# Attention inside a three-layer kernel: four early blocks for the maxima, two of them behind the shifts' transposes, and the values' copy on ACT

## What is computed

```python
q = (x @ Wq + bq).reshape(b, s, HQ, DH).transpose(0, 2, 1, 3)   # HQ = 16 heads, DH = 32
k = x @ Wk + bk                                                # one head of keys for all 16
v = x @ Wv + bv
scores = jnp.einsum('bhsd,btd->bhst', q, k) / scale
attn = jax.nn.softmax(scores, axis=-1)
out = jnp.einsum('bhst,btd->bhsd', attn, v)
out = out.transpose(0, 2, 1, 3).reshape(b, s, HQ * DH)
return out @ Wo + bo
```

## Time and profile before

| | |
|---|---|
| median of 3 runs | 3292.02 us (3288.11 to 3294.11) |
| the profiled execution's own time | 3288.66 us |
| its span, first to last instruction | 3286.9 us |
| attention's groups | from 833 to about 2590 us of the span |
| busy share of the span | PE 86%, DVE 62%, ACT 45%, POOL 67% |
| mean granted clock of TensorE | 0.926 of full speed |

### The profile page before, as it was taken

How to read it: one execution, slowest core, us unless ns; L and a number is a source line. 1 busy time by engine, 2 the same in 40 slices (tenths; PEclk the granted TensorE clock), 3 DMA queues, 4 the chain that set the end, 5 groups by cost and what they waited for, 6 DMA issues and landing times. The chain is left out here.

```text
span 3286.9 us, 50812 instructions
## 1 busy us (share of the span) xinstructions
PE 2812.6 (86%) x15136; PEld 1579.5 (48%) x15136; DVE 2045.0 (62%) x3940; ACT 1481.8 (45%) x2815; POOL 2210.8 (67%) x1392
## 2 busy tenths in 40 slices
PE   7967778398899999999999999999999798777760
PEld 4644444176555454555554544455554355444430
DVE  7943222267788787788787877777875397222222
ACT  3422222153666565566565655665656243222210
POOL 2148888462688787788887877877878222788870
PEclk9989887699999999999999999999999898879885
DMA  6479999894577676676776766757766243999998
GB/s 215 167 210 249 235 243 232 191 278 158 113 161 142 136 159 140 142 153 131 166 142 135 159 138 139 156 116 155 144 124 142 89 166 116 245 235 245 235 197 315
DMA packets 217011, 576.36 MB, mean 175 GB/s; under 512 B 33948, under 2 KB 34972, under 8 KB 192792
## 3 DMA queue, kind: packets, MB, share of 16 engines
q0 software_dynamic: 87296, 343.98, 52.0%
q1 hardware_dynamic: 125208, 220.55, 20.5%
q10 hardware_dynamic: 4224, 8.39, 0.7%
HBM read 230.94 MB, written 155.24 MB: 117 GB/s over the span
## 5 line engine op out<-in xcount | busy, mean ns | idle before, releaser
L1716 DVE TENSOR_REDUCE attention_mx<-attention_pM 128x1 f32<-128x512 f32 x1984 | 1210.8, 680 | 208.7 <-PE attention_pM L1575 192.6
L1520 ACT ACTIVATE attention_prob<-attention_pS 128x512 f32<-128x512 f32 x2048 | 1035.0, 631 | 565.9 <-PE attention_pS L1562 471.3
L1461 POOL TENSOR_TENSOR attention_pair<-attention_prob 128x1024 f32<-128x1024 f32 x380 | 949.5, 2507 | 195.6 <-ACT attention_prob L1520 184.0
L1562 PE MATMUL attention_pS<-attention_qT,prep_kT 128*128 128x512 f32 x2048 | 842.0, 417 | 25.3 <-issue 16.7
L1575 PE MATMUL attention_pM<-prep_kT,attention_qT 96*128 96x512 f32 x1984 | 808.3, 410 | 0.0
L1562 PEld LDWEIGHTS attention_pS<-attention_qT,prep_kT 128*128 128x128 f32 x2048 | 389.2, 191 | 365.8 <-issue 178.0
L1600 PE MATMUL attention_pO<-attention_prob,attention_v 128*32 128x512 f32 x4096 | 492.5, 598 | 0.0
L629 POOL DMA_INDIRECT sum<-experts_res,c_table x256 | 403.7, 1577 | 106.7 <-issue 76.6
L1575 PEld LDWEIGHTS attention_pM<-prep_kT,attention_qT 96*128 96x128 f32 x1984 | 378.5, 192 | 110.4 <-DVE attention_mx L1716 44.4
L755 DVE TENSOR_SCALAR experts_res<-experts_pD,experts_rows 128x512 f32<-128x512 f32 x128 | 90.7, 747 | 422.5 <-DMA sum<-experts_res,c_table 277.3
L658 PE MATMUL experts_pT<-c_ident,experts_rows 128*128 128x128 f32 x1024 | 186.3, 325 | 189.9 <-issue 69.4
(11 more groups left out here) (161 smaller groups left out, 2695.2 us busy)
## 6 DMA issues: line engine op xcount, KB each, us to landing
prep_acc<-attention_pair POOLq DMA_DIRECT2D x96, 1024.0 KB, 7.7
attention_acc<-attention_pair POOLq DMA_DIRECT2D x90, 1024.0 KB, 7.6
experts_wup<-in_L_ffn_w_up_dram SPq DMA_DIRECT2D x128, 256.0 KB
attention_qT<-q_parts SPq DMA_DIRECT2D x96, 256.0 KB
xn_rows<-route_xn SPq DMA_DIRECT2D x16, 1152.0 KB, 6.7
sum<-route_sh SPq DMA_DIRECT2D x16, 1024.0 KB, 4.4
experts_wdn<-in_L_ffn_w_down_dram SPq DMA_DIRECT2D x64, 256.0 KB
q_parts<-prep_acc SPq DMA_DIRECT2D x64, 256.0 KB, 4.4
```

What stands on the lines that cost most here:

```text
L1461: pool.tensor_tensor(to[:, part], prob[2 * n % PROBS][:, part], prob[(2 * n + 1) % PROBS][:, part], ALU.add).then_inc(s_pair, 1)
L1520: act.activation(prob[t % PROBS][:, h * QT:(h + 1) * QT], pS[:, at, :], ACT.Exp).then_inc(s_ex, 1)
L1562: pe.matmul(pS[:, at, :], kT[:, key:key + P], qT[g][:, h, :], start=True, stop=True).then_inc(s_sc, 1)
L1716: dve.tensor_reduce(mx[:, unit, part:part + 1], pM[:, r % RING, :], X, ALU.max).then_inc(s_mr, 1)
```

## The change

`EARLY` becomes 4: two of these blocks go between the four transposes and the values of steps 14 and 15, the other two stay behind these values. `AT_HEAD` loses two blocks. `AT_PAIR` keeps its sum of 56, but pairs 4 and 5 get nine blocks, the ninth right after the eighth, and pair 6 gets six, so that its last two scores follow each other with nothing between. The copy of the values out of pO goes from DVE's head to ACT, between ACT's two shift copies and its first exponential of the next group. The wait for Wo's load moves from ahead of the first loop to `output`. The number of matmuls, reductions and exponentials stays.

```diff
-        EARLY = 2
-        AT_HEAD = (0, 0, 1, 1, 1, 1, 1, 1)
-        AT_PAIR = (8, 8, 8, 8, 8, 8, 8, 0)
+        EARLY = 4
+        AT_HEAD = (0, 0, 0, 0, 1, 1, 1, 1)
+        AT_PAIR = (8, 8, 8, 8, 9, 9, 6, 0)
...
             @block.scalar
+                def copy_o(G, g):
+                    act.wait_ge(s_pv, A + (G + 1) * STEPS)
+                    act.activation(o_raw(g)[:, :], pO[:, :], ACT.Copy).then_inc(s_oc, 1)
...
                             for h in (2, 3):
                                 copy_shift(G + 1, (g + 1) % GPC, h)
+                            copy_o(G, g)
                             for h in range(HG):
                                 exponential(G + 1, 0, h)
...
             @block.tensor
                     if t == 0:
+                        pe.wait_ge(s_wo, A + 16)
                         pe.wait_ge(s_on, A + GPC * (c + 1))
...
-                def early(c, g, ahead):
+                def early(c, g, ahead, blocks):
                     nxt = (g + 1) % GPC
                     pe.wait_ge(s_q[nxt], A + 48 * (c + (2 if nxt == 0 else 1)))
-                    for n in range(EARLY):
+                    for n in blocks:
                         maxima(items_before(c, g), n, n, nxt, ahead, GPC * c + g)
...
                             two_steps(0, 2 * p + 2, () if last else range(AT_PAIR[p]))
+                            if not last and AT_PAIR[p] > 2 * HG:
+                                maxima(base, r, n, nxt, ahead, G)
+                                n, r = n + 1, r + 1
                         elif not last:
                             transposed_shifts(G + 1)
+                            if not before_last:
+                                early(*follower, range(2))
...
                     if not last:
-                        if not (static and c == CHUNKS - 1 and nxt == GPC - 1):
-                            end = static and c == CHUNKS // 2 - 1 and nxt == GPC - 1
-                            early(c + 1 if nxt == 0 else c, nxt, 1 if end else ahead)
+                        if not before_last:
+                            early(*follower, range(2, EARLY))
                         scores(G + 1, nxt, 0, 0, ahead)
...
                 pe.wait_ge(s_init, 1)
                 transposed_shifts(0)
-                early(0, 0, 0)
+                early(0, 0, 0, range(EARLY))
                 scores(0, 0, 0, 0, 0)
-                pe.wait_ge(s_wo, A + 16)
                 chunks(body)(pe)
...
             @block.vector
-                def copy_o(c, g):
-                    dve.wait_ge(s_pv, A + (GPC * c + g + 1) * STEPS)
-                    dve.tensor_copy(o_raw(g)[:, :], pO[:, :]).then_inc(s_oc, 1)
...
-                    if not first:
-                        copy_o(c if g else c - 1, (g - 1) % GPC)
```

More of the change, by code:

```diff
@@ L1509, in _ @@
             def _(act):
-                begin(act, s_ex, s_sha)
+                begin(act, s_ex, s_oc, s_sha)
                 def exponential(G, t, h):
@@ L1651, in group @@
                     ahead = 1 if static and c == CHUNKS // 2 - 1 and nxt == 0 else batch
+                    before_last = static and c == CHUNKS - 1 and nxt == GPC - 1
+                    turn = static and c == CHUNKS // 2 - 1 and nxt == GPC - 1
+                    follower = (c + 1 if nxt == 0 else c, nxt, 1 if turn else ahead)
                     base = items_before(c, g)
@@ L1710, in _ @@
             def _(dve):
-                begin(dve, s_mr, s_mx, s_shift, s_shd, s_dc, s_rec, s_oc, s_lrec, s_lon)
+                begin(dve, s_mr, s_mx, s_shift, s_shd, s_dc, s_rec, s_lrec, s_lon)
                 def maxima(base, r, n):
```

## The result

The changed kernel took 3303.12 us (median of 8 runs, 3295.89 to 3312.39) beside 3290.73 us for the kernel before on the same chips (8 runs, 3286.0 to 3294.11). The ratio is 1.0043, with a 95% interval of 1.0031 to 1.0055: slower by 14 us, at least 10 and at most 18. It is the ratio of the means of these runs; the two medians lie 12.4 us apart. The forecast was 3300, in a range of 3284 to 3310, with "slower" as the likeliest sign.

The account below looks back on a forecast made before the run. PE was taken as the bound, with only its order and short waits left to gain. Terms +6.4 + 0.1 + 4.7 - 1.4 - 0.6 + 0.6 = +9.8 us on 3292.0 give 3301.8, stated as 3300; range 3284 to 3310.

Parts of the forecast that it names:

- slower: The sign given for the whole kernel's measured time: slower 0.58, same 0.30, faster 0.12.
- Pair 4: Pair 4's run in an ordinary group: the ninth block waits for DVE's fifth reduction, which started late, +0.60 us.
- pair 5: Pair 5's run in an ordinary group: the ninth block waits for DVE's fifth reduction, +0.40 us.
- pair 6: Pair 6's run with six blocks: two maxima fewer, but the eighth score waits for ACT's fifth exponential, -0.22 us.
- the shifts' wait: PE's transposes at an ordinary group's end: their wait for DVE's shift instructions goes, -0.50 us.
- the head: From the transposes to the next values: DVE's gain of 1.8 us is given back as idle time, net 0.
- The faster rival: Pairs 4 and 5: ninth blocks don't meet the ring, cost 0.24 us each; about -16 us, 3275 in total; chance 0.11.
- The copy on ACT: Before ACT's first exponential of the next group: the copy costs nothing, with 0.4 us of cover and no table load.
- The term "ordinary": Ordinary groups: +0.60 + 0.40 - 0.22 - 0.50 = +0.28 us each, +6.4 us over 23 groups.
- Projecting groups: Seven projecting groups: pair 4 +0.60, pair 5 +0.40, pair 6 -0.33, no shifts' wait to save; +0.67 us each, +4.7.
- The jumps back: Three group ends with a jump back: the shift of score 0 isn't given back in full, +0.2 us each, estimated.
- The rival that made much of it: POOL's late normalise delays its additions and waiting exponentials, 0.5 us a group, 3315; chance 0.07 for both slower rivals.

Follow-up runs that it names:

- pairs_only: Kernel before with only pairs 4 and 5 at nine blocks and pair 6 at six; early blocks, head and DVE's copy unchanged: 1.0035, 3296.89 us.
- no_ninths: Changed kernel with eight blocks again in all of pairs 0 to 6; four early blocks, shorter head and ACT's copy stay: ratio 1.0006 to the kernel before.
- ninths_12: Changed kernel with the two ninth blocks in pairs 1 and 2 instead of 4 and 5: ratio 1.0024 to the kernel before.
- copy_on_dve: Changed kernel with the copy of the values back on DVE, behind its four early reductions: ratio 1.0036 to the kernel before.
- copy_only: Kernel before with only the copy of the values moved to ACT: ratio 0.9967, 3275.28 us.
- unrolled: Changed kernel with the loops over the chunks written out on PE, ACT, DVE and POOL: ratio 0.9962 to the kernel before.
- recip_early: Changed kernel with DVE's inversion of the denominators behind the fourth instead of the ninth reduction of pair 5: ratio 1.0046 to the kernel before.
- unrolled_recip: unrolled with DVE's inversion of the denominators behind the fourth instead of the ninth reduction of pair 5: ratio 0.9933 to the kernel before.

## Why the prediction was right, and where it was off

**The sign and its mechanism: right.** Pair 4 was forecast at +0.60 us and measured +0.60, pair 5 +0.40 and +0.40, pair 6 -0.22 and -0.22, the shifts' wait -0.50 and -0.50, the head 0 and -0.02, all in ordinary groups inside loops. pairs_only shows that the first four are the layout's doing, and no_ninths that without it nothing is lost that these runs could tell. The method that gave them was one: take each follower's steady pitch, count to the instruction that the ring waits for, and add what a waited load costs.

**The faster rival fell at its own point.** It needed the fifth reduction of a pair done by the eighth block. ninths_12 measured +0.40 in two other pairs as well, so the 0.05 us of margin was enough.

**The head: right, and the reason shown.** DVE's 1.23 us of idle time is the gain given back. copy_on_dve (nothing changes) and copy_only (0.35 us gained where the head still has 14 blocks) show the two sides of it.

**The copy on ACT: right.** It ran in the cover computed for it. ACT's timeline, after:

```profile
1089.57 0.60 ACT L1531 ACTIVATE attention_o_new<-attention_pO 128x512 f32<-128x512 f32 x1 [1.13 <-PE attention_pO L1607]
1090.57 7.96 ACT L1520 ACTIVATE attention_prob<-attention_pS 128x512 f32<-128x512 f32 x16 [0.40 <-PE attention_pS L1568]
```

It ends at T + 3.63, 0.40 us before the first exponential, as worked out. The lines view of the changed kernel still has one table load:

```profile
L1520 ACT ACT_TABLE_LOAD x1 | 1.3, 1283 | 0.0
```

So 31 copies between exponentials switched no table. The rule against mixing functions (the Trainium skill, page "ScalarE: Activation LUTs", section "Table sets: the hidden batching unit") does not bite here, by its own statement that copy is in every set, and the trace agrees.

**The step that failed: one pattern group for 23 ordinary ones.** All rows of the sum came from a chunk inside a loop. In written-out chunks the first exponential starts sooner behind score 0. Of the kernel before, chunk 3, PE and then ACT:

```profile
1692.17 0.87 PE L1562 MATMUL attention_pS<-attention_qT,prep_kT 128*128 128x512 f32 x3
```

```profile
1692.61 7.63 ACT L1520 ACTIVATE attention_prob<-attention_pS 128x512 f32<-128x512 f32 x15 [1.55 <-PE attention_pS L1562]
```

That is 0.44 us; in the loop has 1087.67 for a score at 1087.09, 0.58 us. A follower that is quicker by 0.14 lets pair 6 save 0.36 instead of 0.22 and the head 0.15 instead of 0: 0.60 + 0.40 - 0.36 - 0.50 - 0.15 = -0.01 a group, which is what these windows show. unrolled confirms that the loop makes the difference: there the same groups have 3.58 us in pair 6 and 11.17 us from T to the values. The term "ordinary", with its heads +5.0 us, was therefore +2.9 in 20 groups. Projecting groups likewise: +0.63 in loops, about as forecast (pair 6 saved 0.40 there, not 0.33), +0.35 in the two written-out ones, +3.8 instead of +4.7. Group 0, with the start, was put at -0.5 and gave -1.2, all of it in its head, which varies between 11.6 and 13.4 us over the kernels.

**The jumps back: mis-sized.** +0.2 us each had been allowed; in the two profiled executions they give +4.4 together. This number does not rest on much: over the traces of all kernels with loops, one execution each, the three groups vary between 58.7 and 62.7 us. Part of it is the clock: 0.91 over the 60.04 us shown above is about 11 us at the lower of its two levels, 0.89 over 61.45 us about 14. That it is part of the +14 us is likely, and not shown.

**What stays open of the size.** Groups within chunks account for +5.5 us, with the jumps +10 in these traces; the runs say +14, 10 to 18. Between none and some 8 us lie outside the attention or in its variation: the attention's start alone lies between 824.2 and 836.5 us in the traces of this study, though no kernel changes what stands before it. That the forecast came so near is in part luck: the terms that were too large (ordinary and projecting groups, together 3 us) made up for those that were missing. The chance of the sign does not quite follow from its own rule either: five sixths of 0.58 and 0.07 are 0.55, not 0.58.

**Normalise.** The inversion came later against T by 0.93 us, where 1.0 had been forecast. Normalise was to start at T + 5.6 and end at T + 6.9; in this group it started at T + 5.00, before the change at T + 4.58, and over the ordinary groups of the change at T + 3.7 to T + 5.8. The transfer behind it does not keep a fixed distance from the inversion. POOL's timeline, after:

```profile
1091.54 1.30 POOL L1490 TENSOR_TENSOR attention_o_n<-attention_o_n,attention_d_rec 128x512 f32<-128x512 f32 x1 [0.92 <-DMA attention_d_rec<-d_parts]
```

The rival that made much of it named the right chain, which unrolled shows. In the changed kernel it goes with the spread; a part of a few us in the median is neither shown nor excluded (recip_early).

## What to carry to other kernels

With two followers on rings (here DVE at 0.60 us a block, ACT at 0.49 a score, PE at 0.47 for both), a block is cheap only where its follower is idle, so look for idle time of the follower before moving work, and move no more than the wait needs: one block moved from pair 6 to the head gained 0.7% together with the copy (0.3% alone), while two moved from pair 6 to pairs that were already full lost 0.35%. A part that frees an engine (the copy) is worth its gain only while that engine is the last at that point. Before one pattern group is multiplied by the number of groups, compare one in each kind of code: loop, written out, behind a jump.

## What was not expected of the hardware

A jump back of the loops costs far more than its instructions. PE's row of the first score behind one and two of the next, kernel before:

```profile
1258.15 1.22 PE L1562 MATMUL attention_pS<-attention_qT,prep_kT 128*128 128x512 f32 x2 [5.53 <-issue]
1259.17 0.63 PE L1575 MATMUL attention_pM<-prep_kT,attention_qT 96*128 96x512 f32 x1
1259.59 0.63 PE L1562 MATMUL attention_pS<-attention_qT,prep_kT 128*128 128x512 f32 x1
```

PE issues nothing for 5.53 us, then its blocks start 0.43 us apart instead of 0.235, the granted clock of the window is 0.91 instead of 1.00, and the group is 10 us longer than its neighbours; written out it is 50.25 (unrolled_recip), with the clock at 1.00. The code inside a loop is also slower by itself, 0.14 us from a score to its exponential.

How long the 8 KB write takes goes with how far it is issued behind POOL's accumulating DMA of 1 MB, which itself lands 7.5 us (median) after its issue. In the traces of all fourteen kernels, 30 groups each: 0.1 to 0.3 us behind it, the broadcast followed within 1.6 us in 82 of 113 groups (at most 7.3); 1.1 to 2.4 us behind, after 4.8 to 7.8 us in all 11; 3.1 to 4.0 us behind, after 3.1 to 6.1 us in all 68; more than 5 us behind, after 1.4 to 3.9 us in all 228. No run moved the write alone, so that one causes the other is likely, and not shown.
